# Expert layers with tokens sorted by expert: each token through one expert instead of all four

## What is computed

```python
q, k, v = heads(src @ Wq + bq), ...                     # 16 heads of 8
x = layer_norm(src + attention(q, k, v) @ Wo + bo, ln1_g, ln1_b)
keys = (x @ router_w + router_b)[..., 0]
expert_idx = jnp.remainder(jnp.floor(keys).astype(jnp.int32), N_EXPERTS)   # 4 experts
ff_out = jnp.zeros_like(x)
for e in range(N_EXPERTS):
    h = jax.nn.relu(x @ W1[e] + b1[e])                  # 128 -> 512
    y = h @ W2[e] + b2[e]                               # 512 -> 128
    ff_out = ff_out + jnp.where((expert_idx == e)[..., None], y, 0.0)
return layer_norm(x + ff_out, ln2_g, ln2_b)
# the layer's result, times 0.5, is added to x
```

## Time and profile before

| | |
|---|---|
| median of 3 runs | 1931.81 us (1931.28 to 1939.92) |
| the profiled execution | 1933.48 us, span 1931.3 us |
| TensorE busy | 1437.2 us, 74% of the span |
| DVE / ACT / POOL busy | 70% / 37% / 32% |
| mean granted TensorE clock | 0.864 of full speed |

### The profile page before, as it was taken

One profiled execution on the slowest core, in us unless ns is written; L12 is line 12 of the kernel. 1 busy time (PEld: TensorE's weight loads), 2 busy tenths in 40 slices (PEclk: granted clock), 3 DMA queues, 4 the chain that ended last, 5 costly groups with the idle time before them and its releaser, 6 DMA issues.

```text
span 1931.3 us, 30180 instructions
## 1 busy us (share of the span) xinstructions
PE 1437.2 (74%) x10336; PEld 860.4 (45%) x10336; DVE 1356.9 (70%) x3522; ACT 724.2 (37%) x1329; POOL 615.0 (32%) x464
## 2 busy tenths in 40 slices
PE   3667667656643557988899996665467889989997
PEld 3334334333431223555555664444123455555665
DVE  6699999999873646766776456884665567767554
ACT  1233323333110234555555531222043455555642
POOL 3245445545552201222121123664121122321211
PEclk9887888788755578999999997787576999999999
DMA  4000000000002212211120000001221102210000
GB/s 143 0 1 1 1 0 0 1 0 1 1 2 66 74 61 68 68 51 51 35 68 3 1 1 1 1 0 39 85 75 51 58 28 68 67 52 18 24 12 11
DMA packets 73541, 62.16 MB, mean 32 GB/s; under 512 B 4920, under 2 KB 66488, under 8 KB 73272
## 3 DMA queue, kind: packets, MB, share of 16 engines
q1 hardware_dynamic: 73408, 60.48, 10.0%
HBM read 32.61 MB, written 27.79 MB: 31 GB/s over the span
## 4 chain that ended last, share of the span: by engine, by line
PE 51%; DVE 27%; issue 12%; POOL 4%; DMA 2%; SPq 2%; ACT 1%; DVEq 1%; POOLq 0%; ACTq 0%
PE bank L1073 12%; PE bank L1065 11%; PE bank L1087 7%; DVE DD L1349 6%; PE bank L1103 4%; DVE NM L1578 4%; PE bank L1116 3%; PE bank L955 2%; PE bank L1125 2%; DVE A L1360 2%; PE bank L1136 1%; DVE YB L1491 1%; PE bank L1131 1%; PE bank L1199 1%; POOL rs L582 1%
## 5 line engine op out<-in xcount | busy, mean ns | idle before, releaser
L1578 DVE TENSOR_REDUCE NM<-bank 128x2 f32<-128x512 f32 x512 | 342.5, 685 | 270.2 <-PE bank L1116 269.3
L836 ACT ACTIVATE PBS<-bank 128x512 f32<-128x512 f32 x512 | 289.4, 597 | 393.1 <-PE bank L1103 392.9
L1073 PEld LDWEIGHTS bank<-W,HB 128*128 128x128 f32 x2048 | 264.1, 191 | 157.2 <-issue 135.6
L582 POOL TENSOR_TENSOR rs<-ve,half 128x4 f32<-128x4 f32 x88 | 90.2, 1025 | 707.4 <-DVE ve L1518 587.8
L1073 PE MATMUL bank<-W,HB 128*128 128x128 f32 x2048 | 272.4, 276 | 24.6 <-DVE YB L1491 24.6
L1065 PE MATMUL bank<-XT,W 128*128 128x512 f32 x512 | 284.8, 638 | 1.1 <-ACT HB L808 1.1
L1349 DVE TENSOR_TENSOR_SCAN DD<-bank,I 128x512 f32<-128x512 f32 x192 | 227.1, 1209 | 11.6 <-PE bank L943 9.2
L808 ACT ACTIVATE HB<-bank,W 128x512 f32<-128x512 f32 x256 | 176.5, 690 | 129.3 <-PE bank L1065 128.3
L943 PE MATMUL bank<-STK,SEL 128*128 128x256 bf16 (+1 forms) x512 | 87.5, 281 | 132.3 <-DVE DD L1349 130.7
L1116 PE MATMUL bank<-KS,QS 48*128 48x256 bf16 x1024 | 113.0, 303 | 79.9 <-DVE NM L1578 51.9
L616 POOL TENSOR_TENSOR A<-DD,SS 128x512 f32<-128x512 f32 x64 | 98.6, 1541 | 171.3 <-DVE DD L1349 171.2
(11 more groups left out here) (211 smaller groups left out, 2321.0 us busy)
## 6 DMA issues: line engine op xcount, KB each, us to landing
QS<-scr_q SPq DMA_DIRECT2D x64, 192.0 KB
KS<-scr_k SPq DMA_DIRECT2D x64, 192.0 KB
scr_q<-PQ SPq DMA_DIRECT2D x32, 192.0 KB, 2.2
scr_k<-PQ SPq DMA_DIRECT2D x32, 192.0 KB, 2.2
scr_q<-PQ SPq DMA_DIRECT2D x32, 128.0 KB, 2.1
scr_k<-PQ SPq DMA_DIRECT2D x32, 128.0 KB, 2.1
X<-in_x SPq DMA_DIRECT2D x8, 256.0 KB, 6.6
W<-in_w SPq DMA_DIRECT2D x8, 256.0 KB, 8.3
```

The costliest lines, as they stand in the source:

```text
L582: pool.tensor_tensor(rs_[:, :], ve_[:, :], half[:, 0:ve_.shape[1]], ALU.pow).then_inc(rstd_sem, 1)
L836: act.activation(PB[i % PB_SLOTS][:, :, :], bank[1 + i % 2][:, :].rearrange("p (k t) -> p k t", k=2), ACT.Exp).then_inc(A.e, 1)
L1073: last = pe.matmul(bank[7][:, k * P:(k + 1) * P], HB[e % 2][:, q, k * P:(k + 1) * P], W2[:, e, q, :], start=(q == 0), stop=(q == CH - 1))
L1578: dve.tensor_reduce(NM[:, 2 * b + qt, h:h + 3:2], bank[3 + i % 2][:, :].rearrange("p (u t) -> p u t", u=2), AX_X, ALU.max, negate=True).th ...
```

## The change

Each token now goes through its own expert only. The 512 tokens of a step are sorted into 7 blocks of 128 rows: block e (0 to 3) holds the first 128 tokens of expert e, and blocks 4 to 6 hold what overflows, each block for one expert. As no block has two experts, 3 overflow blocks always suffice (OVER = (512 - 4) // 128).

- `choose` (DVE, slot 26) makes the key as `masks` did, and a one-hot bf16 table. `count_ranks` (TensorE, slot 29) makes each token's rank within its expert by 5 small matmuls. `positions` (DVE, slot 31) makes from these each token's row (POS) and for each overflow block the rows of its weights (WIX), in 14 small operations with 9 links.
- In the next step POOL scatters XS by POS into scr_x (4 indirect DMAs of 128 rows of 512 bytes), SP loads the sorted rows into XD, TensorE turns the 7 blocks at slot 15 into banks 6 and 7, and ACT copies them to XT in slots 15 and 16.
- The experts now stand in slots 17 to 31 alone: `up` for block b in slot 17 + 2b (four products of 128 columns) and `down` one odd slot later (four). ACT takes four Relus of 128x128 a block. Blocks 4 to 6 use weights that POOL gathered into WD by WIX (3 indirect DMAs of 128 rows of 4624 bytes) from a table scr_w, which SP writes once at the start.
- `take` is called twice (4 blocks at slot 26, 3 at slot 1 of the next step). SP stores YB to scr_y, POOL gathers it back by POS into YG (4 indirect DMAs), and DVE adds it to XS at slot 10 in one operation. `masks` and `gather` go.
- KQV shares its memory with the gathered weights. The loop of the middle steps is written out; it ran once. Some semaphores of the attention phase are shared with those of the feed-forward phase. A lead of the next phase moves from slot 26 to slot 28.

```diff
-                        if exp and i == 14:
-                            take(n - 3, 0)
-                        if exp and i == 17:
-                            gather(n - 3, other, 0)
...
+OVER = (N - EXPERTS) // P
+BLOCKS = EXPERTS + OVER
+def first_slot(b):
+    return 17 + 2 * b
...
 # SP
+                    if fin:
+                        sp.wait_ge(E.yused, 2 * (c - 3))
+                        if later(c - 4):
+                            sp.wait_ge(E.back, 64 * (c - 4))
+                        sp.dma_start(scr_y.rearrange("(b p) c -> p b c", p=P), YB[:, :, :]).then_inc(E.ystored, 16)
                     if att:
                         move_max(n - 1, 1, other)
+                    if exp:
+                        sp.wait_ge(E.scattered, 64 * (c - 2))
+                        sp.dma_start(XD[:, :, :], scr_x.rearrange("(b p) c -> p b c", p=P)).then_inc(E.sorted, 16)
 # POOL, behind the power of the step's start
+                    if exp:
+                        pool.wait_ge(E.pos, c - 2)
+                        for t in range(TP):
+                            pool.indirect_dma_start(
+                                out=scr_x, out_offset=bass.IndirectOffsetOnAxis(ap=POS[other][:, t:t + 1], axis=0),
+                                in_=XS[other][:, t, :], in_offset=None).then_inc(E.scattered, 16)
+                    if fin:
+                        pool.wait_ge(E.ystored, 16 * (c - 3))
+                        for t in range(TP):
+                            pool.indirect_dma_start(
+                                out=YG[:, t, :], out_offset=None, in_=scr_y,
+                                in_offset=bass.IndirectOffsetOnAxis(ap=POS[par][:, t:t + 1], axis=0)
+                                ).then_inc(E.back, 16)
+                    if exp:
+                        for k in range(OVER):
+                            pool.indirect_dma_start(
+                                out=WD[:, k, :], out_offset=None, in_=scr_w,
+                                in_offset=bass.IndirectOffsetOnAxis(ap=WIX[other][:, k:k + 1], axis=0)
+                                ).then_inc(E.weights, 16)
 # TensorE
+                def up(p, b):
+                    pe.wait_ge(E.xt, 2 * c + (1 if b < EXPERTS else 2))
+                    if later(c * BLOCKS + b):
+                        pe.wait_ge(E.relu, c * BLOCKS + b)
+                    for k in range(CH):
+                        w = W1[:, b, k * P:(k + 1) * P] if b < EXPERTS else WD[:, b - EXPERTS, k * P:(k + 1) * P]
+                        last = pe.matmul(bank[6][:, k * P:(k + 1) * P], w, XT[:, b * P:(b + 1) * P], start=True, stop=True)
+                    last.then_inc(E.h, 1)
+                def down(p, b):
+                    pe.wait_ge(E.relu, c * BLOCKS + b + 1)
+                    for k in range(CH):
+                        w = W2[:, b, k, :] if b < EXPERTS else WD[:, b - EXPERTS, at:at + P]
+                        last = pe.matmul(bank[7][:, (b % EXPERTS) * P:(b % EXPERTS + 1) * P], HB[b % 2][:, k, :], w,
+                                         start=(k == 0), stop=(k == CH - 1))
+                    last.then_inc(E.y, 1)
 # DVE
+                        if fin and i == 1:
+                            take(n - 4, 1)
+                        if fin and i == 10:
+                            dve.wait_ge(E.back, 64 * (c - 3))
+                            dve.tensor_tensor(AC[:, :, :], XS[par][:, :, :], YG[:, :, :], ALU.add).then_inc(E.acc, 1)
+                        if exp and i == 26:
+                            take(n - 3, 0)
+                        if post and i == 26:
+                            choose(n - 2, par)
+                        if post and i == 31:
+                            positions(n - 2, par)
```

More of the change, by code:

```diff
@@ L350, in program @@
             link_key = sem("exp_link_key")
+            link_pos = sem("exp_link_pos")
             link_ln = sem("exp_link_ln")
+            consts = sem("exp_consts")
+            packed = sem("exp_packed")
+            hot = sem("exp_hot")
+            rank = sem("exp_rank")
+            pos = sem("exp_pos")
+            scattered = sem("exp_scattered")
+            sorted = sem("exp_sorted")
+            weights = sem("exp_weights")
             turned = sem("exp_turned")
@@ L390, in program @@
             sumr = sem("attn_sumr")
+        TOLD = 2 * PAIRS
         schedule, runs, xp = [], {}, 1
@@ L435, in stages @@
                 return [0 <= n - back < PAIRS for back in (-1, 0, 1, 2, 3, 4)]
-            first, last = 4, PAIRS - 2
-            for n in range(start, first):
-                step(n, n % 2, *stages(n))
-            with engine.Fori(0, (last - first) // 2) as it:
-                step(it * 2 + first, 0, *stages(first))
-                step(it * 2 + (first + 1), 1, *stages(first))
-            for n in range(last, PAIRS + 4):
-                step(n, n % 2, *stages(n), between if n > last + 3 else nothing)
+            for n in range(start, PAIRS + 4):
+                step(n, n % 2, *stages(n), between if n > PAIRS + 1 else nothing)
         def short_step(step, n):
@@ new lines, in count_ranks @@
+                def count_ranks():
+                    n = (TP + 1) * EXPERTS
+                    h = hot[:, :, :].rearrange("p t e -> p (t e)")
+                    pe.matmul(bank[0][:, 0:n], below[:, :], h, start=True, stop=False)
+                    for t in range(1, TP + 1):
+                        last = pe.matmul(bank[0][:, t * EXPERTS:n], allone[:, :], h[:, 0:n - t * EXPERTS],
+                                         start=False, stop=(t == TP))
+                    last.then_inc(E.rank, 1)
@@ L1158, in step @@
                         else:
-                            for j in (i - 1, i):
-                                lag, kind, e, k = UNITS[j]
-                                if (post, exp, fin)[lag - 2]:
-                                    unit(n - lag, kind, e, k)
+                            b2 = (i - first_slot(0)) // 2
+                            if exp and 0 <= b2 < BLOCKS:
+                                up(n - 3, b2)
+                            if exp and 0 < b2 <= BLOCKS:
+                                down(n - 3, b2 - 1)
+                            if exp and i == 15:
+                                pe.wait_ge(E.sorted, 16 * (c - 2))
+                                for u, (at, count) in enumerate(((0, EXPERTS), (EXPERTS, OVER))):
+                                    if u == 1 and later(c - 3):
+                                        pe.wait_ge(E.yused, 2 * (c - 3))
+                                    for k in range(count):
+                                        last = pe.transpose(bank[6 + u][:, k * P:(k + 1) * P], XD[:, at + k, :], ident)
+                                    last.then_inc(E.turned, 1)
                         if att and i == 1:
@@ L1544, in masks @@
                     link(dve.tensor_copy(key[2][:, :], kint[:, :]))
-                    for e in range(EXPERTS):
-                        last = dve.tensor_scalar(MK[par][:, e, :], key[2][:, :], float(e), None, ALU.is_equal)
-                    last.then_inc(E.mask, 1)
+                    dve.tensor_tensor(hot[:, 0:TP, :], over(key[2][:, :].unsqueeze(2), [P, TP, EXPERTS]),
+                                      expert_no[:, :, :], ALU.is_equal).then_inc(E.hot, 1)
+                    link.close()
@@ L1648, in step @@
                                   range(TP)).then_inc(E.norm, 1)
-                        if exp and i == 17:
-                            gather(n - 3, other, 0)
-                        if exp and i == 22:
-                            take(n - 3, 1)
-                        if exp and i == 23:
-                            gather(n - 3, other, 1)
                         if fin and i == 25:
```

297 lines of the change are left out of this document (184 added, 113 removed).

## The result

The changed kernel takes 2008.33 us (median of four runs, 2005.79 to 2010.65), the kernel before 1932.80 beside it: 1.0383 times as long, 95% interval 1.0354 to 1.0412. The forecast was 1953 with a range of 1890 to 2010. So the sign and the range held and the size did not: +76 us where +21 was forecast.

The account below looks back on a forecast made before the run. TensorE bounds the kernel, with expert products as filler that keeps its clock up. First phase +6.5, second +13 and constants +2 made +21.5 on 1933.5, so 1955, less 1.7 for the median: 1953 us, range 1890 to 2010.

Parts of the forecast that it names:

- That the old products held the clock up: Slots 0 to 15: expert products were filler keeping TensorE's clock up; without them it behaves as in step 2, 0.72.
- The rival that the clock holds: Slots 0 to 15 take 29.3 us, a steady step saves 3.7, 1875 us in all; chance 0.25.
- Slots 0 to 15 of a steady step, 37 us: Steps 3 to 6, first half: 37.7 us of step 2, less 0.6 and 1, plus 0.9 for XD; 35.6 before.
- Slots 16 to 31, 28.5 us: Second half of a steady step: pairs of slots sum to 29.0, less 0.5 for XS's turn; 25.9 before.
- Four us a step by the sum: Steps 3 to 6 of each phase: 37 + 28.5 = 65.5 us, 4 more than 61.5.
- Steps 8 to 11, -14 and -7.5: Last steps of each phase: step 8 -6 in both, the remainder -8 in the first and -1.5 in the second.
- "-1.5" in the second phase: Steps 9 to 11 there: step 9 -8.7, step 10 +1, bare end 19 for 9.1, the take itself earlier.
- Step 2: +2: Step 2 of each phase: positions and key chain +4, XS's turn and one unit at low clock -2.
- Step 7: +2.5: Step 7 of each phase, no projections: slots 0 to 15 unchanged, slots 16 to 31 28.5 for 25.9.
- DVE's constants, +2: DVE, once: 25 small operations, +2 us.
- POOL's jobs, 1.3 us each and hidden: 11 indirect jobs a step of 1.3 us, covered by POOL's 18 us idle time up to about 1.7 us each.
- The rivals with late transfers: POOL's jobs at 2.5 us each: 2025 us, chance 0.10; at 3.44 us, descriptors held up by DVE: 2105 us, 0.03.

Follow-up runs that it names:

- k3: Kernel before with up units cut to 16 columns and down units to one product of 16 columns: 1960.56 us (one run) against 1934.98.
- k9: Changed kernel with one dead 512-column product in each odd slot from 3 to 13 of steps 2 to 7, chip C: 1897.05 us, 0.9803.
- k10: Changed kernel with `choose` behind reduce 27 instead of 26, chip C: 1966.81 us, 1.0166.
- k12: k11 also without the scatters and the load of XD; TensorE turns XS as it lies: 1958.95 us, 1.0145.
- k14: k12 with dead products in odd slots 3 to 13 and `choose` in slot 27, chip D: 1825.64 us, 0.9427.
- k11: Changed kernel without the store of YB and its gather; the addition reads YB's first four blocks: 2000.06 us, 1.0345.

## Why the prediction was right or wrong

**That the old products held the clock up: right, and shown.** k3 takes them from the kernel before and it slows by 26 us; k9 puts dead ones in the changed kernel and it gains 107 (chip C against chip B, both without the stop). The rival that the clock holds (1875 us, chance 0.25) was wrong as forecast, but its arithmetic was right: with the clock held, slots 0 to 15 take 30.1 us in k9 for the 29.3 worked out.

The Trainium skill (TensorE: Matmul & The Clock Gate, its part on why this matters) warns of idle gaps longer than any here. The prediction weighed that and went by the trace, and the runs agree with the trace: k3 waits 1.37 us at that projection, as the kernel before did, and has 0.63 of the clock for 1.00.

What failed is three terms of the sum, each too small in cost or too large in gain: slots 0 to 15 of a steady step by 21 us in all, slots 16 to 31 by 10, and steps 8 to 11 by 22.

**Slots 0 to 15 of a steady step, 37 us: measured 39.1 to 40.8, 39.6 in the mean.** I took the row of step 2 and then took off 0.6 for a start at full clock and 1 for "a luckier pattern". Neither was there: the half begins with TensorE's wait of 1.97 us for POS, and the mean clock was 0.61, under the 0.68 of the earlier trace rows. The row itself was the lucky one: the same slots of step 2 take 37.7 us in the first phase of the kernel before and 39.6 in the second, and I read only the first. 2.6 us in eight steps are 21 us. The upper bound of 39.5 was nearly the right value.

**Slots 16 to 31, 28.5 us: short by 0.8 to 2.3, 10 us in eight steps.** TensorE's wait behind `choose` was forecast at 2 to 3 us and is 2.27, and the two chains were right within 0.1. What was left out is that the wait costs clock too: slots 28 and 29 took 4.8 to 6.3 us for 3.7, with a unit of 2.07 us in it. k10 moves the chain by one slot and takes 3.6 us from the half; the same half then stands at 1.00.

**Four us a step by the sum, 7.9 measured**, are the two terms above: 31 of the 56 us that the forecast lacked.

**Steps 8 to 11, -14 and -7.5: measured -5.6 and +6.6, the other 22 us.** The ways through memory are not what was missing: in the second phase XD is in 10.6 us after `positions` (11.2 forecast), the first up product of the last pair comes after 12.5 (13.5), and from the last take to the end of the last add to X it is 19.1 (19, though the terms given for it make 18.2). Five other things were, by the two traces; in the order of the list they are 4, 6, 6, 4 and 2 us:

- Step 8 was to go from 43.6 to 37.5 us, -6 in each phase. From its first to its last scores it goes from 45.9 to 40.9 and 43.2. In the second phase its first slots again wait for POS, 2.34 us, and slots 0 to 15 take 21.0 us for 15, at a mean clock of 0.76. The 43.6 was misread besides: that window of the earlier trace rows begins at 1046.40, and the last reduce of step 7 is at 1052.80, the first scores of step 8 at 1054.09.
- From there to the last take the phase was to gain 7.7 us and gained 6.1 and 3.1. In the second phase step 9 takes 34.0 us for 33 (from the end of `positions` to the end of the next), and step 10, given 13.5 + 17 up to the last take, takes 33.2. A block of up, Relu and down takes 2.45 us for the 2.3 forecast, and the first two up units behind the idle stretch run at half clock:

```profile
1963.69 2.09 PE bank L1153 x8
...
1967.08 2.04 PE bank L1153 x8
...
1973.55 1.13 PE bank L1153 x8
```

- The end of the first phase was to be hidden by the next phase's steps. From the last take to the next phase's first reduce it is 181.8 us for 176.3 before, +5.6, and 175.7 in k12, which has no moves.
- "-1.5" in the second phase has 3.7 us more taken off than its terms give (-8.7 + 1 + 9.9 = +2.2), for the earlier take, which these terms hold already.
- From the last add to X to the end of the span it is 5.3 us for 3.0. No term stood for that; it is POOL's late closing signal.

k12 gives the price of both ways: 45.5 us against chip B, 48 by the spans. Most of it was in the sum, so it is what keeps the drain from gaining, and not what the forecast lacked.

**Step 2: +2, measured +3.7 and +4.6**, the same low clock in slots 0 to 15 and the same wait behind `choose` as in the steady steps. **Step 7: +2.5, measured +1.4 and +1.1** at TensorE, while DVE's last reduce of the step is 2.4 and 2.1 us later. DVE's constants, +2, cost nothing visible: the phase's first reduce is at 610.0 us for 609.9. The +2.5 of "the rest" is in steps 0 and 1 of the second phase.

**POOL's jobs, 1.3 us each and hidden: right** (1.26, with 7 us of cover left). The rivals with late transfers (0.13 together) did not come in the runs of the result. On chips A, D and E something like it in size did, by another way: not POOL but TensorE's signals are late, while POOL issues its jobs, at 66 to 70 us for the changed kernel.

The Trainium skill (SBUF — State Buffer, two separate sides) states that GpSimd can be kept from writing descriptors by DVE's work. No run shows it: the 11 jobs of step 5 follow each other with 0.30 us between, whatever DVE does beside them.

**Still open**: what makes TensorE's signals late on some chips. It needs the tokens' moves (in k14 slots 4 and 5 take 3.5 to 4.4 us). It adds more where the other waits of these slots are short: with it slots 4 and 5 take 7 to 12 us, with dead products or without; on chips B and C they take 3.5 us with them and 5.2 without. The traces with it lack a quarter of the DMA landings that the others show (6670 for 8693 in the changed kernel). Whether the profiler has a part in it is not shown. The weight loads' share is open too.

## What to carry to other kernels

Before work is taken from TensorE, look at what the stretch without it is granted: where waits of 1 to 2 us stood between short products here, the work that was removed had been what kept the clock at full, and a few dead products (six a step here, 107 us) were worth more than the saving. Work moved through memory cost nothing here under another pair's work, and its full length, there and back, in the drain. So count a software pipeline's last steps one by one, each between the same marks before and after. And time a change with many small transfers on more than one chip before believing 3%.

## What the runs showed of the hardware that I had not expected

- The same kernel on chips of one kind differed by 3 to 6% with the tokens' indirect moves in it (2004 and 2074; 1897, 2003 and 2018; 1871 and 1966), where the medians of the kernel before differed by 0.3%.
- Products of 16 columns instead of 128 or 512 made a kernel slower, 1935 to 1961 us. The clock of the half that got longer fell from 1.00 to 0.63 (k3).
- One wait of 2.27 us in a stretch that is otherwise full was followed by a unit at the lower clock, 2.07 us for 1.16, and without it (k10) the half is 3.6 us shorter, more than the wait.
- An indirect transfer of 128 rows takes POOL 0.94 to 1.09 us, a plain one on the same queue 0.54, and neither depends on the bytes (64 KB and 592 KB alike). From the start of the last gather's job to its use 3.3 us pass, from the job's end 2.4. The Trainium skill (DMA: Bandwidth & Descriptors, anatomy of one DMA on the gpsimd path) gives 2.0 us fixed and the bytes at 436 GB/s, which makes an estimate of 2.15 us for 64 KB. The trace agrees within 0.25 us if POOL's own 0.94 us are counted beside it.
- A kernel with transfers on POOL's queue closes later: POOL's closing signal came 2.4 us after SP's (5.8 in k11, 0.56 in k12), and 0.03 us after it in the kernel before.
